# Half of the tokens enter the routed loop late: a four-layer transformer block kernel on one core

## The reference

```python
logits = x_flat @ gate_w.T                       # 8 experts
scores = softmax(logits)
w = scores * one_hot(top_k(scores, 2)).sum(1)    # two best experts
gu = einsum('nh,eih->nei', x_flat, experts_gate_up); g, u = gu[..., :176], gu[..., 176:]
out = einsum('neh,ne->nh', einsum('nei,ehi->neh', silu(g) * u, experts_down), w)
out += sigmoid(x_flat @ shared_expert_gate_w.T) * ((silu(x_flat @ shared_gate_w.T) * (x_flat @ shared_up_w.T)) @ shared_down_w.T)
```

## Time and profile before

| | us |
|---|---|
| median of 3 runs | 1480.92 (1480.69 to 1482.76) |
| the profiled execution | 1483.31 |
| its span, from the first to the last instruction | 1481.5 |
| TensorE busy | 1425.8 |
| VectorE busy | 1102.9 |
| ScalarE busy | 977.9 |
| GpSimd busy | 595.4 |

### The profile page before, as it was taken

How to read it: one execution, slowest core, us unless ns; L and a number is a source line. 1 busy time by engine, 2 the same in 40 slices (tenths; PEclk the granted TensorE clock), 3 DMA queues, 4 the chain that set the end, 5 groups by cost and what they waited for, 6 DMA issues and landing times.

```text
span 1481.5 us, 27557 instructions
## 1 busy us (share of the span) xinstructions
PE 1425.8 (96%) x9728; PEld 1154.8 (78%) x9728; DVE 1102.9 (74%) x2433; ACT 977.9 (66%) x1759; POOL 595.4 (40%) x580
## 2 busy tenths in 40 slices
PE   6999999999999999999999999999989999989998
PEld 6888888765666665688888877999867777769998
DVE  3766777688888888477777787687778888866765
ACT  5556666657777777755665667877546666667886
POOL 4466667610000000026666666767501111146674
PEclk8999999999999999999999999999999999999999
DMA  6000000000000000020000002000000000000000
GB/s 180 1 1 1 1 1 1 1 0 1 2 1 1 1 1 1 2 88 1 1 0 1 1 8 79 1 2 1 1 1 2 2 2 1 2 2 1 16 15 29
DMA packets 13320, 16.87 MB, mean 11 GB/s; under 512 B 768, under 2 KB 10496, under 8 KB 12928
## 3 DMA queue, kind: packets, MB, share of 16 engines
q1 hardware_dynamic: 13184, 15.11, 3.3%
HBM read 13.01 MB, written 2.10 MB: 10 GB/s over the span
## 4 chain that ended last, share of the span: by engine, by line
PE 85%; DVE 8%; ACT 3%; issue 3%; DMA 1%; POOL 1%; SPq 0%; DVEq 0%; POOLq 0%; ACTq 0%
PE PS L646 20%; PE PS L674 10%; PE PS L1781 9%; PE PS L1798 8%; PE PS L799 5%; PE PS L819 5%; PE PS L807 4%; PE PS L170 2%; PE PS L1183 2%; PE PS L778 2%; PE PS L1187 2%; PE PS L1158 2%; PE PS L1140 1%; PE PS L1168 1%; PE PS L1207 1%
## 5 line engine op out<-in xcount | busy, mean ns | idle before, releaser
L543 POOL TENSOR_TENSOR RR<-AR,RR 128x512 fp32r<-128x512 f32 x150 | 193.9, 1292 | 470.6 <-ACT RR L574 464.3
L610 ACT ACTIVATE AR<-PS 128x512 f32<-128x512 f32 x224 | 133.9, 598 | 164.9 <-PE PS L646 162.6
L512 DVE TENSOR_TENSOR AR<-AR,PS 128x512 f32<-128x512 f32 x224 | 153.3, 685 | 116.6 <-PE PS L646 113.9
L918 ACT ACTIVATE AR<-PS 128x512 f32<-128x512 f32 x256 | 152.4, 603 | 85.9 <-PE PS L807 85.1
L995 DVE TENSOR_REDUCE AR<-PS 128x2 f32<-128x512 f32 x256 | 172.0, 684 | 21.8 <-PE PS L799 20.9
L646 PE MATMUL PS<-XHI,WG 128*128 128x512 f32 x448 | 177.1, 395 | 0.0
L646 PE MATMUL PS<-XHI,WU 128*128 128x512 f32 x448 | 174.8, 390 | 0.9 <-DVE AR L512 0.7
L516 DVE TENSOR_TENSOR AR<-AR,PS 128x512 f32<-128x512 f32 x224 | 153.8, 687 | 8.1 <-POOL RR L543 0.5
L1876 ACT ACTIVATE PS<-PS 128x1024 f32<-128x1024 f32 x96 | 96.8, 1009 | 58.9 <-PE PS L1781 58.6
L1781 PE MATMUL PS<-XHI,SL 128*128 128x256 f32 x576 | 133.6, 287 | 2.1 <-DVE XTR L1945 2.1
L2053 POOL CAST SL<-ZW 128x1024 fp32r x96 | 100.1, 1043 | 85.7 <-PE PS L1798 85.1
(11 more groups left out here) (281 smaller groups left out, 3465.4 us busy)
## 6 DMA issues: line engine op xcount, KB each, us to landing
X<-in_x SPq DMA_DIRECT2D x4, 512.0 KB, 6.6
out_x<-X SPq DMA_DIRECT2D x4, 512.0 KB, 3.2
AR<-in_w SPq DMA_DIRECT2D x1, 1792.0 KB, 11.5
XT<-in_w SPq DMA_DIRECT2D x1, 1608.0 KB, 6.5
AR<-in_zone_up SPq DMA_DIRECT2D x6, 256.0 KB, 5.3
AR<-in_zone_down SPq DMA_DIRECT2D x6, 256.0 KB, 5.6
XT<-in_sel SPq DMA_DIRECT2D x1, 896.0 KB, 6.1
SM<-in_small SPq DMA_DIRECT2D x1, 857.5 KB, 7.2
```

The source lines that it names most:

```text
L512: v.tensor_tensor(PRD[:, m % 2, :], SIL[:, m % 2, :], bank(2 + m % 2), ALU.mult).then_inc(S.prod, 1)
L543: g.tensor_tensor(HL[k % 3], GAT[:, m % 2, :], HH[k % 3].bitcast(F32), ALU.subtract).then_inc(S.h_lo, 1)
L610: act.activation(SIL[:, m % 2, :], bank(m % 2), ACT.Silu).then_inc(S.silu, 1)
L918: act.activation(PT[:, g % 2, k, 2 * jp:2 * jp + 2, :], bank(2 + m % 2).rearrange("p (j q) -> p j q", j=2), ACT.Exp, scale=SC0).then_inc(S ...
```

## The change

Only chunks 0 to 3 (HALF) are normalised, turned, copied and put through the gate at the begin of a routed stage. After that TensorE makes the products of tiles 0 and 1 of chunk 0, 14 keep_busy calls, and turns the gate rows of chunks 0 to 3 in two rounds. Chunks 4 to 7 are normalised by ScalarE alone; chunk 4 and 5 ahead of the loop, the others in it. All late chunks are turned into bank 7, in the loop, and their copies, low parts and logits stand at written-out tiles of chunks 0 and 1 (late_pe, late_act, late_dve). The gate chain of the second half of the tokens lies in chunk 2, in pieces; its gate rows are turned one chunk at a time in chunks 3 and 4 (rounds 2 to 5 of wt_turn). The chain's steps are each on half as many elements, and the first pick is written straight to OH, so that one copy is gone. Waits are added for bank 7 and for XN. The first loop's products wait for the low parts of WG and WU only (G.split at 1), its first down product for all (G.split at 2). ACC moves to the end of the area of H3; the order in which zone weights are split changes with it, and zone 6 waits for the last chunk's turning back. The zone weights' loads wait for the second half's gate weights.

The diff, cut to its core:

```diff
-        HIGHS = (0, 6, 7, 1, 2, 3, 4, 5)
-        POOL_LO = (6, 2, 7)
+        HIGHS = (0, 7, 1, 2, 3, 4, 6, 5)
+        POOL_LO = (7, 2, 6)
...
+        HALF = NC // 2
+        ACC = nc.alloc_sbuf_tensor_at("ACC", [P, 512], F32, offset=experts_at + 4 * (6 * MT0 * P + 2 * P + 1024))[:, :]
...
+        def turn_in(n, c):
+            S, D = ST[n], counts(n)
+            pe = nc.tensor
+            if c < HALF:
+                wait(pe, S.xlo, c - 3, D.xlo)
+            elif c == HALF:
+                pe.wait_ge(S.wt_lo, D.wt_lo + 2)
+            else:
+                pe.wait_ge(S.lg_dve, D.lg_dve + c)
+            if c == NC - 1:
+                pe.wait_ge(S.x_new, D.x_new + 1)
+            if on_act(n) < TPC and c < HALF:
+                pe.wait_ge(S.xn, D.xn + c + 1)
+            pe.wait_ge(S.xna, D.xna + c + 1)
+            for t in range(TPC):
+                last = pe.transpose(turned_in(c)[:, t * P:(t + 1) * P], XN[:, c % 2, t, :], ident)
+            last.then_inc(S.tr, 1)
+        def logits(n, c):
+            S, D = ST[n], counts(n)
+            pe = nc.tensor
+            pe.wait_ge(S.xt, D.xt + c + 1)
+            if c >= HALF:
+                pe.wait_ge(S.xlo, D.xlo + c + 1)
+            for t in range(TPC):
+                last = pe.matmul(logits_in(c)[:, t * GC:(t + 1) * GC], XTC[:, c % 2, t * P:(t + 1) * P], T.gw,
+                                 start=True, stop=True)
+            last.then_inc(S.lg_pe, 1)
+        def normed_in(n, c, tiles):
+            S, D = ST[n], counts(n)
+            act = nc.scalar
+            if tiles[0] == 0:
+                wait(act, S.tr, c - 1, D.tr)
+            for t in tiles:
+                k = c * TPC + t
+                last = act.activation(XN[:, c % 2, t, :], X[:, k, :], ACT.Identity, scale=RSTD[:, k:k + 1],
+                                      bias=NBIAS[:, k:k + 1])
+            if c >= HALF and tiles[-1] == TPC - 1 or c < HALF:
+                last.then_inc(S.xna, 1)
+        def copies_in(n, c):
+            S, D = ST[n], counts(n)
+            act = nc.scalar
+            act.wait_ge(S.tr, D.tr + c + 1)
+            wait(act, S.lg_pe, c - 1, D.lg_pe)
+            act.activation(XTC[:, c % 2, :], turned_in(c), ACT.Copy).then_inc(S.xt, 1)
+            act.activation(XHI[:, c * 512:(c + 1) * 512], turned_in(c), ACT.Copy).then_inc(S.xhi, 1)
...
+        def gate_exps(n, h):
+            S, D, ts = ST[n], counts(n), half(h)
+            act = nc.scalar
+            act.wait_ge(S.p_max, D.p_max + h + 1)
+            act.activation(PR[:, ts], PR[:, ts], ACT.Exp).then_inc(S.p_exp, 1)
+            act.activation(SG[:, ts], LG[:, ts, E0], ACT.Exp, scale=-1.0).then_inc(S.p_exp, 1)
...
+        def gate_best(v, n, ch, h, k):
+            ts, src = half(h), P2 if k else PR
+            ch.link(v.tensor_reduce(T1[:, ts], src[:, ts], AX.X, ALU.max))
+            ch.link(v.tensor_tensor(EQ[:, ts], src[:, ts], bh(T1, h, E0), ALU.is_equal))
+            ch.link(v.tensor_tensor(EQ[:, ts], EQ[:, ts], rev.unsqueeze(1).to_broadcast([P, NT // 2, E0]), ALU.mult))
+        def gate_first(v, n, ch, h, k):
+            ts = half(h)
+            ch.link(v.tensor_reduce(T2[:, ts], EQ[:, ts], AX.X, ALU.max))
+            if k == 0:
+                ch.link(v.tensor_tensor(OH[:, ts], EQ[:, ts], bh(T2, h, E0), ALU.is_equal))
+                ch.link(v.scalar_tensor_tensor(P2[:, ts].rearrange("p t e -> p (t e)"), OH[:, ts].rearrange("p t e -> p (t e)"),
+                                               -2.0, PR[:, ts].rearrange("p t e -> p (t e)"), ALU.mult, ALU.add))
+            else:
+                ch.link(v.tensor_tensor(EQ[:, ts], EQ[:, ts], bh(T2, h, E0), ALU.is_equal))
+                ch.link(v.tensor_tensor(OH[:, ts], OH[:, ts], EQ[:, ts], ALU.add))
...
+        def wt_place(r):
+            return (bank(4 + 2 * r, 2), slice(r * 1024, (r + 1) * 1024)) if r < 2 else (bank(7), slice((r + 2) * 512, (r + 3) * 512))
+        def wt_turn(n, r):
+            S, D = ST[n], counts(n)
+            pe = nc.tensor
+            pe.wait_ge(S.w_all, D.w_all + (1 if r < 2 else 2))
+            o, at = wt_place(r)
+            if r in (2, 4):
+                pe.wait_ge(S.x_new, D.x_new + 3 + (r - 2) // 2)
+            if r in (3, 5):
+                pe.wait_ge(S.wt_lo, D.wt_lo + r)
+            for t in range(at.start // P, at.stop // P):
+                last = pe.transpose(o[0:NG0, t * P - at.start:(t + 1) * P - at.start], WALL[:, t, :], ident)
+            last.then_inc(S.wt_pe, 1)
...
+        def late_pe(n, c, m):
+            k = MT0 * c + m
+            for i, at in enumerate((1, 5, 10, MT0 + 8)):
+                if k == at:
+                    turn_in(n, HALF + i)
+            for i, at in enumerate((4, 8, 13, MT0 + 11)):
+                if k == at:
+                    logits(n, HALF + i)
+            for i, at in enumerate((3 * MT0 + 8, 3 * MT0 + 11, 4 * MT0 + 8, 4 * MT0 + 11)):
+                if k == at:
+                    wt_turn(n, 2 + i)
+        def late_act(n, c, m):
+            k = MT0 * c + m
+            for i, at in enumerate((2, 6, 11, MT0 + 9)):
+                if k == at:
+                    copies_in(n, HALF + i)
+            for i, at in enumerate((3, 7)):
+                if at <= k < at + TPC:
+                    normed_in(n, HALF + 2 + i, [k - at])
+            if k == 2 * MT0 + 2:
+                gate_exps(n, 1)
+            for i, at in enumerate((3 * MT0 + 9, 3 * MT0 + 12, 4 * MT0 + 9, 4 * MT0 + 12)):
+                if k == at:
+                    wt_high(n, 2 + i)
+        def late_dve(n, ch, c, m):
+            v = nc.vector
+            k = MT0 * c + m
+            for i, at in enumerate((3, 7, 12, MT0 + 10)):
+                if k == at:
+                    low(n, HALF + i)
+            for i, at in enumerate((5, 9, MT0, MT0 + 12)):
+                if k == at:
+                    logits_out(n, HALF + i)
+            if k == 2 * MT0:
+                gate_logits(v, n, ch, 1)
+            if k == 2 * MT0 + 2:
+                gate_share(v, n, ch, 1)
+            if k in (2 * MT0 + 5, 2 * MT0 + 9):
+                gate_best(v, n, ch, 1, (k - 2 * MT0) // 9)
+            if k in (2 * MT0 + 6, 2 * MT0 + 11):
+                gate_first(v, n, ch, 1, (k - 2 * MT0) // 11)
+            if k == 2 * MT0 + 13:
+                gate_weights(v, n, ch, 1)
+            for i, at in enumerate((3 * MT0 + 10, 3 * MT0 + 13, 4 * MT0 + 10, 4 * MT0 + 13)):
+                if k == at:
+                    wt_low(n, 2 + i)
...
+            keep_busy(pe, bank(3), 18 if n else 20)
+            for c in range(HALF):
                 if c > 0:
-                    keep_busy(pe, bank(c % 4), 4)
...
-            for c in range(NC):
-                turn(c)
+                    wait(pe, S.xlo, c - 3, D.xlo)
+                    keep_busy(pe, turned_in(c), 4)
+                turn_in(n, c)
                 if c > 0:
-                    logits(c - 1)
-            logits(NC - 1)
-            pe.wait_ge(S.xlo, D.xlo + NC)
-            keep_busy(pe, bank(0), 38 if n else 46)
...
+            mine = range(on_act(n))
+            normed_in(n, 0, mine)
+            normed_in(n, 1, mine)
+            for c in range(HALF):
+                copies_in(n, c)
+                if c + 2 < HALF:
+                    normed_in(n, c + 2, mine)
+            normed_in(n, HALF, range(TPC))
...
+            gate_exps(n, 0)
+            normed_in(n, HALF + 1, range(TPC))
+            for r in range(2):
+                wt_high(n, r)
...
+            def gates(c, s):
+                pe.wait_ge(S.wt_lo, D.wt_lo + (c // 2 + 1 if c < HALF else c - 1))
+                wait(pe, S.gated, MT0 * c if s else MT0 * (c - 1) + SHARED, D.gated)
+                pe.matmul(bank(4 + s), SEL[:, s * P:(s + 1) * P], WTS[:, bass.ds(c * 512, 512)],
+                          start=True, stop=True).then_inc(S.w_pe, 1)
...
+                if k == 0:
+                    pe.wait_ge(G.split, 2)
+                    pe.wait_ge(S.wt_lo, D.wt_lo + 2)
...
+                    if not first or m > 1:
+                        up(c, m)
+                    if m in (0, SHARED):
+                        gates(c, m // SHARED)
+                    if first and m == 1:
+                        pe.wait_ge(S.wt_lo, D.wt_lo + 2)
...
+            pe.wait_ge(G.split, 1)
+            up(0, 0)
+            up(0, 1)
+            pe.wait_ge(S.lg_dve, D.lg_dve + HALF)
+            keep_busy(pe, bank(7), 14)
+            for r in range(2):
+                wt_turn(n, r)
...
-            sp.wait_ge(F.w_all, B.w_all + 1)
+            sp.wait_ge(F.w_all, B.w_all + 2)
...
+                    if e == 6:
+                        act.wait_ge(ST[n - 1].back, counts(n - 1).back + NC)
...
+            last.then_inc(G.split, 1)
```

More of the change, by code:

```diff
@@ L358, in normed @@
                 last.then_inc(S.xn, 1)
[L360 to L368, removed]
@@ new lines, in logits_in, with low, logits_out @@
+        def logits_in(c):
```

(40 more changed lines are left out.)

139 lines of the change are left out of this document (65 added, 74 removed).

## The result

The changed kernel takes 1490.80 us (median of 4 runs, 1490.34 to 1491.36) against 1480.81 (4 runs, 1480.25 to 1482.76) on the same chip: ratio 1.006, interval 1.0048 to 1.0071. That is 10 us slower, where 1.8 us slower was forecast, and above the range's upper end of 1488. The profiled execution took 1491.36 us for a span of 1489.6, 8.1 more than the span before. The medians differ by more than the two spans, since the profiled execution of the kernel before was 2.5 us slower than its median and this one 0.6.

What follows compares the result with a forecast made beforehand. TensorE, busy 96% of the span, was taken as the bound. Begins' gains less added work, stalls and clock, 11.2 + 4.3 - 2 x 5.9 - 4.2 - 1.3 = -1.8 us, gave a median of 1482.7 us; range 1475.5 to 1488.

Steps and rivals of the forecast that it cites:

- Begins: Starts of both routed stages: late logits end 4.3 us earlier in the first, 11.2 us in the second.
- The term that stood for the clock: Second stage's ramp: low TensorE clock over two or three microseconds of products costs 1.3 us, between 0 and 4.
- First stage, what ends its begin: First stage: keep_busy passes end at 47.4 us, gate rows at 47.6 or 40.1; gate matmul near 51 either way.
- TensorE's added work: Routed loops: late turns, logits and gate-row transposes add 7.2 us a stage, 5.9 of it behind the ramp.
- Waits of the loops: Both routed loops: TensorE stalls 1.9 us (second stage), 0.7 (first), plus 1.5 for both: 4.2 us, bounds 0 and 9.
- Each stands one tile or more behind what it waits for ... 0.4 us or more of room: Late turns and logits on TensorE in the loop: enough room, so priced at nothing, except the first logits.
- the 2.5 us of room: Chunk 2 of the loops: TensorE stalls only once VectorE's product is over 2.5 us late.
- The term I had there: Chunk 2: TensorE waits on VectorE's late product, 1.9 us in the second stage, 0.7 in the first.
- The port lock: Second gate chain: one group in four loses 1.1 us beside GpSimd, half passed to TensorE; 1.5 us for both stages.
- The rival "port lock": Chunk 2: every group reading two SBUF operands waits for or delays GpSimd; 8.6 us of stall, 1487.1 us; chance 0.15.

Runs made afterwards that it cites:

- all three edits: Changed kernel with chunk 5 and 6 turns one tile later, second gate chain dealt out (Exps behind acc_copy), keep_busy passes moved: 1477.39 us, ratio 0.9971; rerun 1477.91, 0.9970.

## Why the prediction was wrong

- **Begins: right in the sum, in part by luck.** 4.2 and 9.8 us for 4.3 and 11.2. The 1.4 us missing are in the second stage: the clock fell at 621 to 625 us in this profile, so 36 keep_busy passes took 5.15 us where they took 4.18, four transposes before them took longer too, and the first turn came 1.4 us late. No term stood for this. The term that stood for the clock, 1.3 us for the ramp, came at 0.3 at most: the clock was low from 645 to 653, but from the gate rows to the late logits it is 13.6 us, where 13.3 was forecast without it. The two errors nearly cancel: 14.0 us in all for 4.3 + 11.2 - 1.3 = 14.2.
- **First stage, what ends its begin: right, and it pointed at a gain I did not see.** I had both the passes (47.4) and the gate chain (47.6 or 40.1) near the end. The passes ended at 48.10, the chain at 43.96. All eleven steps of two SBUF operands were held up beside GpSimd, 0.63 to 1.24 us each instead of 0.30, and so were two of one operand:
```profile
35.01 1.24 DVE L480 SCALAR_TENSOR_TENSOR AR<-AR 128x128 f32<-128x128 f32 x1
36.28 0.29 DVE L471 TENSOR_REDUCE AR<-AR 128x16 f32<-128x128 f32 x1
...
41.75 1.11 DVE L489 TENSOR_SCALAR AR<-AR 128x16 f32<-128x16 f32 x1
```
  From the late end of the logits the chain took 16.6 us, where 16.2 was worked out with GpSimd's hold. It was early only because it began 4.0 us early, as the clock stayed up from 14 to 27 us; begun at 31.4, it would have ended at 48.0, with the passes.
- **TensorE's added work: right.** 6.2 us a stage for 5.9.
- **Waits of the loops: the step that failed.** 4.2 us for both loops where 10.3 came, above the upper bound of 9. It failed in three parts:
  1. "Each stands one tile or more behind what it waits for ... 0.4 us or more of room" is false for the turn of chunk 5: it stands in tile 5 of chunk 0, and so does logits_out of chunk 4 that it waits for, behind that tile's two products on VectorE, which run later than TensorE's tile 5. 1.2 us a loop; shown by the later turns.
  2. acc_copy was left out. I followed the late silu to VectorE's product and asked when TensorE would miss it, but not what else is queued on ScalarE behind the Exps and who waits for that: the down product, three tiles behind, does not have the 2.5 us of room that VectorE's product has. 1.87 us a loop; shown by the copies for Exps and by the Exps in tile 2 again. The term I had there, waits on VectorE's product in chunk 2 (2.6 us in all), came only as one of 0.5 us, in the second loop.
  3. VectorE's lag does not end with chunk 2. TensorE waits for its product in chunk 3's first tile; and ScalarE's copy of the gated product waits for VectorE, so next_normed (L723) and acc_copy (L716), which stand behind that copy, are late, and with them TensorE's next_turn and a down product in chunk 3. 1.3 + 0.5 us in the first loop, 1.4 + 0.5 and the 0.5 of part 2 in the second; shown by the copies for Exps, where it stays, and by the dealt-out chain, where it goes.
- **The port lock** was priced too low, at 1.1 us of VectorE's time in one group of four. The two groups of the first pick had steps of 0.28 to 0.29 us in the first loop (one of 0.64 in the second), but in the second pick two steps of each group were held, 0.64 and 1.27, 0.57 and 1.35 us: 2.7 us over 0.29 each. In the kernel with the Exps behind acc_copy the two longest took 1.29 and 1.35. The Trainium skill (SBUF — State Buffer, section "Who interferes with whom") says that a VectorE instruction with two SBUF inputs contends with a GpSimd instruction that reads SBUF, and the later one waits out the other. The trace agrees: the step that began at 145.62 ended at 146.97, just after GpSimd's (145.53 + 1.29 = 146.82). The rival "port lock" was nearest in size (8.6 us of waits, 1487.1 us), and its condition, more than one group in four, was met, but it was not the mechanism of most of the loss: of 10.3 us of waits, 4.2 are the dense chain with its late VectorE; 2.4 and 3.7 are the other two waits, for which it has no part. Within the 4.2 no run takes the lock out. An estimate from the timeline: VectorE had no gap from 133.83 to 147.69 and TensorE idled 0.5 us for it in chunk 3's first tile, so without the 2.7 us of holding it would have been there in time. The lock alone does no harm either: in the dealt-out chain it still costs VectorE some 2.3 us in the first loop and 1.7 in the second, and TensorE waits for none of it.
- **Ways out not weighed.** The forecast took the sum of gains and costs as given by the change. It was worth a ratio of 1.0060 as placed, 0.9988 with the same work at other tiles, and 0.997 with the idle passes moved too.

## What to carry to other kernels

When work is put into a tuned loop, list for each engine what stands behind each added instruction and who waits for it, down to the once-per-chunk copies: slack in the mean (0.6 us of a tile on VectorE, 0.9 on ScalarE here) says nothing of an instruction that is queued behind a burst of 3 us. Deal a chain out at a step or two a tile, put a table switch just behind the last copy that TensorE waits for, and put a wait on another engine a full tile later than the tile that carries its source. A begin that a change shortens has a new set of fillers to tune, idle passes among them.

## What the runs showed of the hardware

- A copy of 16 elements a partition, one SBUF operand, also took 1.27 us beside GpSimd's subtraction in the changed kernel (L491, at 150.99; GpSimd's ran from 150.93 for 1.29), and 0.19 in the dealt-out one.
- A step of one operand was held as well in the first begin: 1.11 us for a TENSOR_SCALAR of 16 elements (L489, at 41.75), 0.16 at 150.50 with GpSimd idle. The step of 1.30 us in the earlier trace rows, on which the price of the lock was read, is also a TENSOR_SCALAR.
- Two switches of ScalarE's table with two small Exps between them took 122.86 - 119.82 = 3.04 us, the sum of their durations (1.28 + 0.31 + 0.22 + 1.28) within 0.05: nothing is lost beside the loads.
- TensorE's granted clock also fell to 0.50 (1.2 GHz) where idle passes filled the long waits. In the kernel with idle passes it fell at 48 us, behind waits of 1.3, 1.5 and 0.7 us with transposes between. In the first profile of all three edits the passes left 2.56 us before the products; it fell from 40 to 44 us, and then stayed at 1.00 over waits of 1.5 and 0.7 us. In the second profile of that kernel 0.84 us were left, it held over the products, and was low from 49 to 52.
- A wait just before is not the whole of it. In the kernel with idle passes the clock was at 0.50 from 28 to 31 us, while TensorE had run since 18.1 us with no gap over 0.2 us; in the first profile of all three edits it was at 1.00 there, in the same code. The 84 passes took 11.27 us and 9.64. The kernel with idle passes:
```profile
28.00:29.00 1.00, 1.00 (x7) 1.00 (x7) 0.42 (x1) 0.98 (x2) 1.00 (x2) 0.50 0.00 0
```
  So a gain that hangs on where the clock falls differs from execution to execution, and no run here tells what decides it.
